# Handing a second layer-2 product pair to GpSimd in the last four blocks of a recommendation tower

## The reference

```python
for W in (W0, W1, W2):                       # 3 layers, 64 features out of each
    xk = relu(einsum('bmd,bhd,mhk->bkd', x0, xk, W))
    outs.append(sum(xk, axis=2))             # sum over d
h = concat(outs, dense_ctx)                  # 192 + 16
y = relu(relu(h @ W_top1 + b1) @ W_top2 + b2) @ W_top3
```

## Time and profile before

| | us |
|---|---|
| median of 3 runs | 646.18 (644.88 to 648.17) |
| profiled execution, span from first to last instruction | 645.9 |
| TensorE busy | 598.9 (93%) |
| VectorE busy | 586.6 (91%) |
| GpSimd busy | 443.4 (69%) |
| ScalarE busy | 355.7 (55%) |

### The profile page before, as it was taken

One profiled execution on the slowest core, in us unless ns is written; L12 is line 12 of the kernel. 1 busy time (PEld: TensorE's weight loads), 2 busy tenths in 40 slices (PEclk: granted clock), 3 DMA queues, 4 the chain that ended last, 5 costly groups with the idle time before them and its releaser, 6 DMA issues.

```text
span 645.9 us, 8924 instructions
## 1 busy us (share of the span) xinstructions
PE 598.9 (93%) x3046; PEld 248.2 (38%) x3046; DVE 586.6 (91%) x398; ACT 355.7 (55%) x665; POOL 443.4 (69%) x305
## 2 busy tenths in 40 slices
PE   4377999699999999999999999999999999999988
PEld 3242432233543344433543343433443343434434
DVE  5466999699999999999999999999999999999873
ACT  0155480755747293846657382927666582828361
POOL 5656787488888888487878788787878460706220
PEclk9579899799999999999999999999999999999999
DMA  6699969967898949976897959885998869691000
GB/s 181 144 225 260 213 183 232 259 137 149 210 213 244 213 130 236 269 170 144 245 213 223 212 149 238 251 188 114 252 214 244 179 215 215 206 214 31 1 1 1
DMA packets 60175, 119.82 MB, mean 186 GB/s; under 512 B 15271, under 2 KB 33734, under 8 KB 60054
## 3 DMA queue, kind: packets, MB, share of 16 engines
q1 hardware_dynamic: 49414, 114.69, 72.0%
q0 software_dynamic: 7584, 1.96, 3.5%
q10 hardware_dynamic: 3152, 2.86, 1.6%
HBM read 115.27 MB, written 5.25 MB: 187 GB/s over the span
## 4 chain that ended last, share of the span: by engine, by line
PE 58%; DVE 23%; issue 10%; ACT 4%; another core or an unknown queue 3%; DMA 1%; DVEq 0%; SPq 0%; ACTq 0%
PE acc L968 50%; DVE z_dve L529 14%; DVE z_dve L549 4%; PE psm L1071 2%; PE psm L1079 2%; ACT xq L717 1%; DVE x0b L698 1%; ACT xq L771 1%; PE acc L983 1%; DVE x0b L652 1%; DMA x_rot<-in_tbl_dram 1%; DVE z_dve L642 1%; ACT xs L717 1%; DVE zacc L583 1%
## 5 line engine op out<-in xcount | busy, mean ns | idle before, releaser
L529 DVE TENSOR_TENSOR z_dve<-xq,x0b 128x2048 f32<-128x2048 f32 x179 | 398.7, 2279 | 17.6 <-issue 11.4
L968 PE MATMUL acc<-z_dve,w_cin 128*64 128x512 f32 x1688 | 390.3, 602 | 16.6 <-DVE z_dve L549 8.5
L472 POOL TENSOR_TENSOR z_pool<-x0b,xs 128x2048 f32<-128x2048 f32 x45 | 205.3, 4566 | 96.8 <-ACT xs L717 93.8
L447 POOL DMA_INDIRECT emb<-in_tbl_dram,ids_all x224 | 218.3, 975 | 75.7 <-issue 61.5
L968 PEld LDWEIGHTS acc<-z_dve,w_cin 128*64 128x64 f32 x1688 | 130.4, 138 | 241.5 <-issue 191.0
L754 ACT ACTIVATE xq<-acc 64x512 f32<-64x512 f32 x64 | 36.5, 570 | 130.6 <-PE acc L968 105.5
L549 DVE TENSOR_TENSOR z_dve<-xq,x0b 128x1024 f32<-128x1024 f32 x64 | 76.1, 1216 | 13.3 <-ACT xq L754 10.7
L968 PE MATMUL acc<-z_pool,w_cin 128*64 128x512 f32 x360 | 86.3, 593 | 0.0
L717 ACT ACTIVATE xs<-acc 64x512 f32<-64x512 f32 x124 | 73.4, 592 | 1.7
L771 ACT ACTIVATE xq<-acc 32x512 f32<-32x512 f32 x128 | 72.2, 564 | 1.9
L725 ACT ACTIVATE xq<-acc 32x512 f32<-32x512 f32 x128 | 72.2, 564 | 1.7
(11 more groups left out here) (99 smaller groups left out, 249.5 us busy)
## 6 DMA issues: line engine op xcount, KB each, us to landing
x0b<-x0t SPq DMA_DIRECT2D x120, 512.0 KB
x_rot<-x0t SPq DMA_DIRECT2D x60, 512.0 KB
x_rep<-x0t SPq DMA_DIRECT2D x15, 512.0 KB
x0b<-x0t SPq DMA_DIRECT2D x16, 256.0 KB
emb<-in_tbl_dram,ids_all POOLq DMA_INDIRECT x224
x0t<-emb_t SPq DMA_DIRECT2D x28, 128.0 KB
w_cin<-in_L_rec_W_dram SPq DMA_DIRECT2D x16, 64.0 KB
x_lo<-x0t SPq DMA_DIRECT2D x15, 64.0 KB
```

The source lines that it names most:

```text
L447: nc.gpsimd.indirect_dma_start(out=rows[:, D * f:D * f + D], out_offset=None, in_=tables[f], in_offset=bass.IndirectOffsetOnAxis(ap=ids_al ...
L472: nc.gpsimd.tensor_tensor(z_pool[:, n % ZP_SLOTS, :, :], x0b[b % 2][:, 2 * j:2 * j + 2, :], xs[l - 1][:, :].unsqueeze(1).broadcast_to([P, ...
L529: nc.vector.tensor_tensor(z_dve[:, base % Z_SLOTS, :, :], in0.unsqueeze(1).broadcast_to([P, 2, N]), in1, ALU.mult).then_inc(z_made, 1)
L968: ins = nc.tensor.matmul(acc[l][K * side:K * side + K, :], weights[c], z[:, c, NH * side:NH * side + NH], start=start and c == 0, stop=sto ...
```

## The change

`pool_l2(b)` returns (2, 3) for the last four blocks, (3,) before that. So GpSimd makes the products NAT 2 and NAT 3 of layer 2 and VectorE six instead of seven. TensorE's order of layer 2 in those blocks has NAT 2 in fifth and NAT 3 in seventh place.

```diff
     def pool_l2(b):
 
-        return (3,)
+        return (2, 3) if b >= BLOCKS - 4 else (3,)
...
     def l2_order(b):
 
+        if b >= BLOCKS - 4:
+            return [(NAT, 0), (NAT, 1), (SWP, 0), (SWP, 1), (NAT, 2), (SWP, 2), (NAT, 3), (SWP, 3)]
         return [(NAT, 0), (NAT, 1), (NAT, 2), (SWP, 0), (NAT, 3), (SWP, 1), (SWP, 2), (SWP, 3)]
```

## The result

The changed kernel took 656.75 us (median of four runs, 655.58 to 657.80) against 645.89 of the kernel before in the same comparison (644.88 to 648.17): 1.0158 times as long, 95% interval 1.0124 to 1.0192, and +10.9 us between the medians. Two later comparisons gave 1.0131 (1.0107 to 1.0154) and 1.0150 (1.0106 to 1.0194). It is slower by some 8 to 11 us.

The account below looks back on a forecast made before the run. ScalarE's chain, 10.9 us from layer 1 to SWP 0, was taken as the bound, not VectorE. 645.9 + 7.1 for later products + 2.3 for the clock = 655.3, forecast as 655.5 us with the median's 0.3; range 651.5 to 658.3.

Parts of the forecast that it names:

- The chain of 10.9 us: Layer 2, blocks 12 to 15: ScalarE's spreads and copy keep SWP 0 from starting sooner than 10.91 us after layer 1.
- 2.20 us a block less the lateness: Layer 2 ends 2.20 us later per block, less SWP 0's lateness against ScalarE: +1.95, +1.53, +1.74, +2.20 in blocks 12 to 15.
- What hides the rest: Blocks 12 to 15: GpSimd's second product, later x0b reload, sum_d and add_relu cost nothing; GpSimd's cover 5.3 and 4.1 us.
- The clock: TensorE's gaps before SWP 0 in blocks 12, 14 and 15 send its clock to half: +2.3 us, bounds 0 and 5.1.
- The price of a fall, 1.1: Each clock fall at the long gaps costs 1.1 us: 3.4 us at half clock, a third inside the gap.
- The number, 2.1: Clock falls expected in or after the three long gaps, from chances of 0.5, 0.8 and 0.8.
- The sum: Whole kernel: 645.9 + 7.1 + 2.3 = 655.3 us, with the median 0.3 above the profiled execution; forecast 655.5 us.
- The Trainium skill's rule: TensorE's gaps before SWP 0: idle between matmul bursts halves the clock, making the change worse than the +7.1 us pair count.

Follow-up runs that it names:

- scalar_swap: The changed kernel with ScalarE doing `x2_swp` before `x2_pool` in tiles 6 and 7; 1.0128 times the kernel before.
- the two filled kernels: The changed kernel with NAT 1 repeated on zero weights before SWP 0 in blocks 12, 14 and 15, in two series; 1.0111 and 1.0112 times the kernel before.

## Why the prediction was right, point by point

- **The chain of 10.9 us.** Right to 0.01 us in all four blocks, and shown by scalar_swap, not only read.
- **2.20 us a block less the lateness.** From layer 0 of block 12 to that of block 13 the change takes 547.14 - 509.10 = 38.04 us against 36.09: +1.95, as predicted. To block 14: 36.16 against 34.90, +1.26, predicted 1.53 - 0.3 = 1.23. From there to the end: 63.74 against 58.59, +5.15; less the fall 3.94, predicted 1.74 + 2.20. Sum without the clock +7.15, predicted +7.1; the two filled kernels, which have no falls, show +7.15 and +7.16.
- **What hides the rest.** GpSimd's longer work, the later reloads, sum_d and add_relu cost nothing, as said. VectorE waits 4.41 us ahead of layer 1 of block 15 (the row below), 0.99 before the change, and TensorE still finds its products: it has no idle in brackets in that layer 1.

```profile
605.16 11.08 DVE L531 TENSOR_TENSOR z_dve<-xq,x0b 128x2048 f32<-128x2048 f32 x5 [4.41 <-issue]
```

- **The clock.** The price of a fall, 1.1, was nearly right (1.2), but not for its reason: no third of the fall lies in the gap, it begins behind it, and what makes it cheaper than 1.7 is the wait for SWP 1 that it takes up. The number, 2.1, was too high for the profiled executions: each has one, and the gap of block 15 came through whole, though it is as long as block 14's. So this term is 1.2 us in the trace in place of 2.3. Over all executions, by the mean clocks above, it is an estimated 1.1 falls on one chip and 2.1 on the other.
- **The sum.** 655.5 was forecast (655.3 + 0.3, as the prediction has it, is 655.6) and 656.75 measured, but that they are so near is partly luck. The forecast's difference was 9.4 us; the traces give 8.4 and the medians of the first comparison 10.9 (its interval, 1.0124 to 1.0192, is about 8.0 to 12.4 us and holds all three). The two measured differences fit together through the profiled executions. The prediction set the span of one against the median of the device times, and these aren't the same measure: in the runs after, the device time is 1.8 to 2.4 us over the span of the same execution. So the profiled execution of before, whose own device time is not known, took about 647.7 us or more, some 1.8 above its median, while that of the change (656.24) was 0.5 under its median. 8.5 us between the spans, 1.8 and 0.5 make 10.8. What the profiled execution of before lost against its median is not shown.
- **The Trainium skill's rule** ("TensorE: Matmul & The Clock Gate", the table "Why this matters for your kernels") that idle gaps between bursts send the clock back agrees in direction: block 14's gap of 2.7 to 2.9 us had a fall in all four traces that have it, and filling the gaps took the falls away. Block 15's gap of 2.87 us, without a fall in five of six traces, shows that such a gap doesn't always do it.

## What to carry to other kernels

A product less on a busy engine is worth nothing if what it waits for next is another engine: look at the wait that ends just before the instruction you want earlier, here 0.26 us for ScalarE, small only because the product you want to remove hides it. When TensorE's order is changed, ask what fills the time until the first operand of the next kind can exist, and keep the ready pairs in front of it, not behind. Filling an unavoidable gap with work of no effect can be worth a microsecond, for the clock: 1.2 us in the traces here.

## What the runs showed of the hardware

The same kernel before took 645.9 and 647.0 us in two series and 633.8 and 633.9 in the other two. The two of 633.8 and 633.9 ran on one chip and the one of 647.0 on another; for that of 645.9 the chip is not on record. From the traces of the change, almost all of the difference arises before block 12: its layer 0 starts at 509.10 or 508.71 us in the slower ones and at 495.14 in the faster one, and from there to the matmuls of line 1109 all agree to 0.01 us. Their rows of w_sym lie 4.2 us apart at 44 us of the span (44.23 and 40.02), 14.2 at 225 and 14.0 from 260 on, so the loss is in the first 225 us. Whether the chip is the cause was not tried. It is why a ratio is always taken within a series here.
